# VectorE's adjacency offsets: one fifteen-word register load a round against four loads of up to four words

## The chip, the cores and the metric

The kernel runs on one core of one Trainium2 chip. The metric is the device time of one execution in microseconds. Before the change the median of three runs is 1594.96 us (1593.28 to 1598.29).

## The reference, cut to what matters

There are 3125 nodes with 128 features and 100000 edges, sorted by destination. Two graph layers follow one another, each with a residual and a layer norm.

```python
# layer 0: max over the incoming edges of a linear message
msgs = z[edge_dst] @ Wd + z[edge_src] @ Ws + edge_weight[:, None] * ww[None, :] + bm
agg = jax.ops.segment_max(msgs, edge_dst, num_segments=n)
x = _layernorm(x + relu(z @ W1a + agg @ W1b + b1) @ W2 + b2)
# layer 1: two SAGE convolutions, each with the mean over the incoming edges
agg = jax.ops.segment_sum(x[src], dst, num_segments=n)
mean = agg / jnp.maximum(deg, 1.0)[:, None]
x = _layernorm(x + conv2(relu(conv1(x))))
```

## The kernel before, in words

The kernel has three parts in time. First a setup sorts out where edges and nodes lie. Then the gather pass `gather_pass(0)` computes the segment maximum of layer 0, and beside it builds the adjacency matrix as counts in SBUF (`adj`, bf16). Then the dense tail runs the layers; the second layer's sums are matmuls with that adjacency matrix.

The change is in the gather pass. It has 49 rounds (`ROUNDS`). A round has 16 steps (`RING`), in four blocks of four (`NB`, `BS`). In each block:

- GpSimd gathers four sets of 128 rows by indirect DMA (L651), after ScalarE has copied the indices (L486).
- ScalarE computes the weighted part of four messages (L496).
- VectorE waits for the gathered rows (`landed`, L826) and for ScalarE (`weighed`, L828), adds the two for the whole block (L830), waits for the end of its own addition (`summed`, L831), and then runs four steps. A step is one running maximum (L841); steps are chained by the semaphore `stepped` (L840).

In the first 47 rounds (`PROUNDS`) the first 15 steps (`RP`) of a round also take a pair each, 705 pairs in all. A pair stands for one batch of 256 edges and one window of ten destination nodes. VectorE and ScalarE make one-hot matrices for it (L855 and L857 on VectorE, L526 and L535 on ScalarE), TensorE multiplies them into a PSUM bank (L1123), and three steps later (`LAG`) VectorE adds the product into 250 columns of the adjacency matrix (`add_product`, L861 to L866). Which columns these are is known only at run time: the start is a number that VectorE's sequencer reads into a register. The numbers lie in SBUF in `offw`, 16 words to a round (`OFFW`), fifteen of them used.

The load of these registers is L836, `values_load_multi_w_load_instructions`, in `turn` of VectorE's `gather_pass`. It stands in the loop over the steps, where `j % OFFS == 0`, ahead of the wait and the step L841 of the same j. With `OFFS = 15` that is j = 0 alone: one load of fifteen words a round, behind the wait for `summed` of the first block. After the 47 rounds another load of three words (L879) serves the last three products. One further register load is used in the trace as a measure: L283 reads one word on each engine to choose the form of the second layer.

All of the order is written out by hand; each engine executes its own list, and the loops over the rounds are real loops with a register counter. So the column of `nlo`, `key`, `keep` and the waited values are computed by register instructions on the engine's sequencer. In the trace these stand as DVEq, VectorE's sequencer.

The constants that matter:

```python
RP = 15
LAG = 3
OFFS = 15
OFFW = 16
```

Of the kernel before, what the change touches and what calls it, by code (L numbers as in the profile page):

```python
# [52 lines left out]
RP = 15  # L53
PR = 5
LAG = 3
OFFS = 15
OFFW = 16
WINDOWS = ("COLS times a pair's window, which is the number of NWIN ordered window starts at or before the pair, less "
           "one; the first of them is pair 0")
# [25 lines left out]
def gnn_kernel(nc, x, src, dst, w, Wm, bm, W1, b1, W2, b2, W1lT, b1l, W1rT, W2lT, b2l, W2rT, out):  # L85
# [16 lines left out]
    with ctx:  # L102
# [96 lines left out]
        offw = off.rearrange("p r c -> p (r c)")  # L199
# [492 lines left out]
        def _(dve):  # L692
# [123 lines left out]
            def gather_pass(q):  # L816
# [6 lines left out]
                def turn(i, first, pairs):  # L823
                    offs = []
                    for b in range(NB):
                        dve.wait_ge(landed[b], q * ROUNDS * BS * 16 + 16 * BS * i + 16 * BS)  # L826
                        if q == 0:
                            dve.wait_ge(weighed, i * NB + b + 1)  # L828
                            part = runs[:, b * BS:(b + 1) * BS, :]
                            nc.vector.tensor_tensor(part, part, gath[:, b * BS:(b + 1) * BS, :], ALU.add).then_inc(summed, 1)  # L830
                            dve.wait_ge(summed, i * NB + b + 1)  # L831
                        elif not first:
                            dve.wait_ge(dumped[b], q * ROUNDS * 16 + 16 * i)
                        for j in range(b * BS, (b + 1) * BS):
                            if pairs and j < RP and j % OFFS == 0:
                                offs += nc.values_load_multi_w_load_instructions(  # L836
                                    offw[0:1, bass.ds(i * OFFW + j, OFFS)], engines=[mybir.EngineType.DVE],
                                    min_val=0, max_val=(NWIN - 1) * COLS, skip_runtime_bounds_check_because=WINDOWS)[1]
                            if not (first and j == 0):
                                dve.wait_ge(stepped, q * CHUNK + i * RING + j)  # L840
                            nc.vector.scalar_tensor_tensor(  # L841
                                runs[:, j, :], runs[:, (j - 1) % RING, :], mask[:, bass.ds(i * RING + j, 1)],
                                (runs if q == 0 else gath)[:, j, :], op0, op1).then_inc(stepped, 1)
                            if pairs and j < RP:
                                one_hots(i, j, first)
                                if not (first and j < LAG):
                                    add_product(offs[j], i * RP + j - LAG, (j - LAG) % PR, first and j == LAG)

                def one_hots(i, j, first):
                    s = j % PR  # L850
                    if not (first and j < PR):
                        dve.wait_ge(paired, i * RP + j - PR + 1)
                    for u in range(SUB):
                        if j not in BY_ACT:
                            nc.vector.tensor_scalar(hot_l[:, s, u * P:(u + 1) * P], niota_l[:, :],  # L855
                                                    nlo[:, u, bass.ds(i * RP + j, 1)], None, ALU.is_equal)
                        last = nc.vector.tensor_scalar(hot_d[:, s, u * COLS:(u + 1) * COLS], iota_d[:, :],  # L857
                                                       key[:, u, bass.ds(i * RP + j, 1)], None, ALU.is_equal)
                    last.then_inc(made_d, 1)

                def add_product(at, n, s, alone):  # L861
                    dve.wait_ge(paired, n + 1)
                    if not alone:
                        dve.wait_ge(added, n)
                    a = adj[:, bass.ds(at, COLS)]
                    nc.vector.tensor_tensor(a, bank[s][:, 0:COLS], a, ALU.add).then_inc(added, 1)  # L866

                if q == 0:
                    dve.wait_ge(zeroed[0], 16)
                turn(0, True, q == 0)  # L870
                if q == 0:
                    with dve.Fori(1, SAFE) as i:
                        turn(i, False, True)
                    with dve.Fori(SAFE, SAFE + ZROUNDS) as i:
                        dve.wait_ge(zeroed[1], i * 16 - (SAFE - 1) * 16)
                        turn(i, False, True)
                    with dve.Fori(SAFE + ZROUNDS, PROUNDS) as i:
                        turn(i, False, True)
                    offs = nc.values_load_multi_w_load_instructions(  # L879
                        offw[0:1, PROUNDS * OFFW:PROUNDS * OFFW + LAG], engines=[mybir.EngineType.DVE], min_val=0,  # L880
                        max_val=(NWIN - 1) * COLS, skip_runtime_bounds_check_because=WINDOWS)[1]
                    for k in range(LAG):
                        add_product(offs[k], PAIRS - LAG + k, (PAIRS - LAG + k) % PR, False)
# [390 lines left out]
```

## Time and profile before

| | |
|---|---|
| median of three runs | 1594.96 us |
| lowest and highest | 1593.28 and 1598.29 us |
| the profiled execution's own time | 1589.41 us |
| its span in the profile | 1587.6 us |
| VectorE busy | 1087.8 us |
| ScalarE busy | 884.1 us |
| GpSimd busy | 845.0 us |
| TensorE matmul busy | 835.7 us |
| granted TensorE clock, mean | 0.622 of full speed |

The profile comes from one execution. Its span is from the first to the last instruction; the execution's own time is 1.8 us longer. Busy time counts work on data only: register loads, register arithmetic, branches and waits are not in it. They are seen as DVEq rows of the chain that ended last and of a single line's view, and as idle time of the engine, where "issue" names idle time that no semaphore of another instruction explains.

### The profile page before, as it was taken

To read this page: it belongs to the slowest core of one execution; us is meant where nothing else is said; L and a number is where in the kernel's file an instruction comes from. 1 tells how busy PE (TensorE), PEld (TensorE's weight loads), DVE (VectorE), ACT (ScalarE), POOL (GpSimd) and SP (SyncE) were. 2 spreads that over 40 slices of the span, in tenths; PEclk is the share of its full clock that TensorE was granted. 3 is DMA by queue.
4 is the path that set the end of the run, shared out by engine and by line. 5 is a ranking of instruction groups with operands and counts; after the bars stand their busy time and mean duration, and the time that the engine had idled before them with its cause. 6 is when DMAs were issued, how large, how long until landed. Compare 5 with 4: busy or idle time off the path is not lost.

```text
span 1587.6 us, 27890 instructions
## 1 busy us (share of the span) xinstructions
PE 835.7 (53%) x3528; PEld 428.8 (27%) x3528; DVE 1087.8 (69%) x3961; ACT 884.1 (56%) x2856; POOL 845.0 (53%) x851
## 2 busy tenths in 40 slices
PE   0473444443444444444444444444409969999898
PEld 0441000000000000000000000000006748887687
DVE  3368888888888888898888898888843341112433
ACT  0117787777787777777777877777711130001200
POOL 1056777777777777777777777777755000000000
PEclk9785555555555555555555555555556579999899
DMA  2583444444443333333333333333342231111211
GB/s 81 168 296 119 134 155 146 143 149 130 140 150 96 94 95 101 95 94 101 94 96 94 101 96 94 99 96 96 99 129 76 67 92 40 41 40 41 65 34 30
DMA packets 114997, 163.01 MB, mean 103 GB/s; under 512 B 20330, under 2 KB 74013, under 8 KB 114954
## 3 DMA queue, kind: packets, MB, share of 16 engines
q1 hardware_dynamic: 86276, 99.13, 18.5%
q0 software_dynamic: 27952, 63.24, 14.5%
q8 instruction: 19, 0.31, 0.1%
q10 hardware_dynamic: 726, 0.13, 0.1%
q14 instruction: 24, 0.20, 0.0%
HBM read 79.07 MB, written 63.28 MB: 90 GB/s over the span
## 4 chain that ended last, share of the span: by engine, by line
DVE 36%; PE 21%; issue 17%; DVEq 15%; DMA 6%; SPq 3%; ACT 1%; POOL 1%; POOLq 0%; ACTq 0%
PE bank L1229 12%; DVE late L857 11%; DVE rings L830 8%; DVE adj_w L866 7%; DVEq L836 6%; DVE rings L841 5%; DVEq L857 3%; DVE late L855 2%; DMA adj_w<-dst_d,adj_w 2%; DVEq L841 2%; PE bank L1202 2%; SPq L312 2%; DMA dst_d<-adj_w 2%; PE bank L1169 1%; DVEq L866 1%
## 5 line engine op out<-in xcount | busy, mean ns | idle before, releaser
L651 POOL DMA_INDIRECT rings<-zs_d,idx x784 | 790.3, 1008 | 270.8 <-issue 246.9
L1123 PE MATMUL bank<-late 128*128 128x250 bf16 x1410 | 421.3, 402 | 602.5 <-DVE late L857 591.5
L526 ACT ACTIVATE late<-late 128x128 bf16<-128x128 bf16 x1128 | 367.5, 388 | 24.1
L857 DVE TENSOR_SCALAR late<-late 128x250 bf16<-128x250 bf16 x1410 | 374.1, 310 | 0.0
L841 DVE SCALAR_TENSOR_TENSOR rings<-rings,keep 128x128 f32<-128x128 f32 x784 | 269.6, 344 | 140.4 <-issue 103.8
L1123 PEld LDWEIGHTS bank<-late 128*128 128x128 bf16 x1410 | 93.2, 111 | 930.2 <-DVE late L857 581.4
L866 DVE TENSOR_TENSOR adj_w<-bank,adj_w 128x250 f32 x705 | 287.4, 408 | 0.9 <-DVE adj_w L866 0.4
L535 ACT ACTIVATE late<-late 128x256 bf16<-128x256 bf16 x564 | 223.8, 405 | 90.3 <-PE bank L1123 90.3
L496 ACT ACTIVATE rings<-ww,late 128x128 f32<-128x128 f32 x784 | 250.3, 390 | 1.6 <-DVE rings L841 1.6
L1229 PE MATMUL bank<-rings,adj_w 128*128 128x384 bf16 (+1 forms) x1250 | 214.3, 332 | 20.7 <-DVE rings L1007 20.7
L1229 PEld LDWEIGHTS bank<-rings,adj_w 128*128 128x128 bf16 (+1 forms) x1250 | 180.9, 149 | 51.5 <-DVE rings L1007 29.2
L830 DVE TENSOR_TENSOR rings<-rings 128x512 f32<-128x512 f32 x196 | 132.8, 678 | 9.2 <-DMA rings<-zs_d,idx 9.1
L577 ACT ACTIVATE late<-bank,cols 128x256 f32<-128x256 f32 (+1 forms) x39 | 16.8, 464 | 181.4 <-PE bank L1170 181.4
L486 ACT COPY idx<-src_i 128x4 int32 (+1 forms) x196 | 37.7, 193 | 139.8 <-DVE rings L841 103.5
L965 DVE COPY late<-bank 128x256 f32<-128x256 f32 (+1 forms) x13 | 5.4, 415 | 116.4 <-PE bank L1205 116.4
L855 DVE TENSOR_SCALAR late<-late 128x128 bf16<-128x128 bf16 x282 | 76.3, 272 | 0.0
L1021 DVE TENSOR_REDUCE late<-bank 128x128 f32<-128x384 f32 (+1 forms) x50 | 26.8, 554 | 63.2 <-PE bank L1229 61.0
L642 POOL DMA_INDIRECT adj_w<-dst_d,adj_w x25 | 23.8, 951 | 85.4 <-DMA dst_d<-adj_w 69.0
L557 ACT ACTIVATE sd<-mv,eps 128x2 f32<-128x2 f32 (+1 forms) x26 | 7.7, 297 | 93.3 <-DVE mv L923 93.3
L783 DVE TENSOR_SCALAR_CACHE_REDUCE adj_w<-adj_w 128x784 f32<-128x784 f32 x25 | 25.7, 1029 | 33.6 <-DMA adj_w<-dst_d,adj_w 33.4
L476 ACT COPY adj_w<-bank 128x256 f32<-128x256 f32 (+1 forms) x13 | 4.7, 365 | 70.5 <-PE bank L1081 48.3
L913 DVE TENSOR_TENSOR late<-rings,bank 128x256 f32<-128x256 f32 (+1 forms) x13 | 5.3, 411 | 44.5 <-PE bank L1146 33.5
(157 smaller groups left out, 600.0 us busy)
## 6 DMA issues: line engine op xcount, KB each, us to landing
run_d<-rings SPq DMA_DIRECT2D x196, 256.0 KB, 2.1
adj_w<-zeros SPq DMA_DIRECT2D x16, 980.0 KB
rings<-zs_d,idx POOLq DMA_INDIRECT x784
adj_w<-zeros SPq DMA_DIRECT2D x1, 3920.0 KB, 24.4
late<-x_d SPq DMA_DIRECT2D x24, 128.0 KB, 2.3
xT_d<-adj_w SPq DMA_DIRECT2D x12, 128.0 KB, 6.8
zs_d<-adj_w SPq DMA_DIRECT2D x12, 128.0 KB, 6.5
late<-xT_d SPq DMA_DIRECT2D x12, 128.0 KB, 2.2
```

The costliest lines, as they stand in the source:

```text
L496: last = nc.scalar.activation(runs[:, b * BS + j, :], ww[:, :], ACT.Copy, scale=w_s[:, bass.ds(i * RING + b * BS + j, 1)])
L526: last = nc.scalar.activation(a[:, u * P:(u + 1) * P], iota_l[:, :], ACT.Square, bias=nlo[:, u, bass.ds(i * RP + j, 1)])
L535: nc.scalar.activation(hot_l[:, s, :], sq[:, n % 2, :], ACT.Relu, bias=1.0, scale=-1.0).then_inc(made_l, 1)
L651: pool.indirect_dma_start(gath[:, j, :], None, table, bass.IndirectOffsetOnAxis(ap=idx[:, j:j + 1], axis=0), compute_op=ALU.bypass).then_i ...
L830: nc.vector.tensor_tensor(part, part, gath[:, b * BS:(b + 1) * BS, :], ALU.add).then_inc(summed, 1)
L836: offs += nc.values_load_multi_w_load_instructions(offw[0:1, bass.ds(i * OFFW + j, OFFS)], engines=[mybir.EngineType.DVE], min_val=0, max_ ...
L841: nc.vector.scalar_tensor_tensor(runs[:, j, :], runs[:, (j - 1) % RING, :], mask[:, bass.ds(i * RING + j, 1)], (runs if q == 0 else gath)[ ...
L855: nc.vector.tensor_scalar(hot_l[:, s, u * P:(u + 1) * P], niota_l[:, :], nlo[:, u, bass.ds(i * RP + j, 1)], None, ALU.is_equal)
L857: last = nc.vector.tensor_scalar(hot_d[:, s, u * COLS:(u + 1) * COLS], iota_d[:, :], key[:, u, bass.ds(i * RP + j, 1)], None, ALU.is_equal)
L866: nc.vector.tensor_tensor(a, bank[s][:, 0:COLS], a, ALU.add).then_inc(added, 1)
L1123: last = nc.tensor.matmul(bank[s][:, 0:COLS], hot_l[:, s, u * P:(u + 1) * P], hot_d[:, s, u * COLS:(u + 1) * COLS], start=u == 0, stop=u = ...
L1229: return nc.tensor.matmul(bank[ADJ_BANKS[t % 3]][0:k, 0:3 * F], adj_v[:, t * P:t * P + k, h], parts[:, h, :], start=h == 0, stop=h == NT - 1)
```

## The change

The group of a load becomes four words instead of fifteen, and the last load of a round takes the three that remain. So in each of the 47 rounds there are four loads, of 4, 4, 4 and 3 words, at j = 0, 4, 8 and 12. Each is the first step of a block, so that each load stands behind that block's wait for `summed`. The 3-word load at L879 stays as it is.

```diff
-OFFS = 15
+OFFS = 4
...
                             if pairs and j < RP and j % OFFS == 0:
                                 offs += nc.values_load_multi_w_load_instructions(
-                                    offw[0:1, bass.ds(i * OFFW + j, OFFS)], engines=[mybir.EngineType.DVE],
+                                    offw[0:1, bass.ds(i * OFFW + j, min(OFFS, RP - j))], engines=[mybir.EngineType.DVE],
                                     min_val=0, max_val=(NWIN - 1) * COLS, skip_runtime_bounds_check_because=WINDOWS)[1]
```

## Rows read from the trace of the kernel before

**Rows 1.** The profile's first two parts: busy time of the engines, and the 40 slices.

```profile
span 1587.6 us, 27890 instructions
PE 835.7 (53%) x3528; PEld 428.8 (27%) x3528; DVE 1087.8 (69%) x3961; ACT 884.1 (56%) x2856; POOL 845.0 (53%) x851
...
DVE  3368888888888888898888898888843341112433
...
PEclk9785555555555555555555555555556579999899
```

**Rows 2.** Busy time by stretch: stretch, its length, PE, PEld, DVE, ACT, POOL, clock, DMA.

```profile
129.00:1148.00 1019.00, 420.68 (x1408) 93.03 (x1408) 883.49 (x3333) 808.87 (x2636) 760.93 (x754) 0.50 0.36 112
1148.00:1182.00 34.00, 1.04 (x3) 0.32 (x3) 18.90 (x46) 8.14 (x29) 21.78 (x22) 0.50 0.34 106
```

**Rows 3.** VectorE's waits from 129 to 1148 us: total us, times, longest.

```profile
DVE rings L841 <- issue: 103.8, 47, 2.3
DVE rings L841 <- DVE rings L830: 31.4, 138, 0.2
DVE adj_w L866 <- issue: 0.2, 1, 0.2
```

**Rows 4.** Timeline of VectorE: two loads one round apart, and a block without one.

```profile
608.06 0.35 DVE L841 SCALAR_TENSOR_TENSOR rings<-rings,keep 128x128 f32<-128x128 f32 x1 [2.22 <-issue]
...
613.23 0.35 DVE L841 SCALAR_TENSOR_TENSOR rings<-rings,keep 128x128 f32<-128x128 f32 x1 [0.23 <-DVE rings L830]
...
629.73 0.35 DVE L841 SCALAR_TENSOR_TENSOR rings<-rings,keep 128x128 f32<-128x128 f32 x1 [2.22 <-issue]
```

**Rows 5.** Chain that ended last, 626 to 630 us: start, us, what.

```profile
626.82 0.69 DVE rings L830
627.52 0.03 issue
627.55 0.08 DVEq L836
627.63 0.03 issue
627.66 1.93 DVEq L836
629.59 0.05 issue
629.64 0.05 DVEq L841
```

**Rows 6.** Line L836: durations ns min/median/max, first and last start.

```profile
L836 DVEq TENSOR_LOAD <-late x47: 1800/1922/2050, 129.5 to 1127.6; - x47
L836 DVEq FUSED_REGOPS  x46: 64/81/81, 149.3 to 1127.5; - x46
```

**Rows 7.** Lines L879 and L283, same columns: register loads of three and one words.

```profile
L879 DVEq TENSOR_LOAD <-late x1: 767/767/767, 1147.9 to 1147.9; - x1
...
L283 DVEq TENSOR_LOAD <-large x1: 439/439/439, 1283.2 to 1283.2; - x1
```

**Rows 8.** Timeline of VectorE around the three-word load.

```profile
1147.89 0.40 DVE L866 TENSOR_TENSOR adj_w<-bank,adj_w 128x250 f32 x1
1148.22 0.33 DVE L841 SCALAR_TENSOR_TENSOR rings<-rings,keep 128x128 f32<-128x128 f32 x1
1148.90 0.42 DVE L866 TENSOR_TENSOR adj_w<-bank,adj_w 128x250 f32 x1 [0.34 <-PE bank L1123]
```

**Rows 9.** Groups by line, 129 to 1148 us: busy, mean ns, idle before and releasers.

```profile
L651 POOL DMA_INDIRECT rings<-zs_d,idx x754 | 760.9, 1009 | 261.6 <-issue 239.0 <-ACT idx L486 22.6
L1123 PE MATMUL bank<-late 128*128 128x250 bf16 x1408 | 420.7, 402 | 602.1 <-DVE late L857 591.1 <-issue 8.1 <-ACT late L535 1.6
...
L535 ACT ACTIVATE late<-late 128x256 bf16<-128x256 bf16 x564 | 223.8, 405 | 90.3 <-PE bank L1123 90.3
...
L486 ACT COPY idx<-src_i 128x4 int32 (+1 forms) x188 | 36.3, 193 | 92.6 <-DVE rings L841 92.6
```

**Rows 10.** Timeline of GpSimd, one gather with the pause before it.

```profile
611.22 0.97 POOL L651 DMA_INDIRECT rings<-zs_d,idx  x1 [0.30 <-issue]
```

## The prediction, made before the changed kernel was run

> **What bounds the kernel now.** Read the slices first: VectorE is at eight or nine tenths in nearly all slices of the long middle, while TensorE's clock there stands at half, the lower of its two levels, 1.2 GHz [rows 1]. Then cut that middle out: from 129 to 1148 us, 1019 us long, VectorE works 883.5 us, more than any other engine [rows 2]. Its 135.5 us of idle time have two causes only [rows 3]: 103.8 us ahead of 47 maxima L841 with no releaser ("issue"), and 31.4 us ahead of 138 others, behind the block's addition L830. No wait for GpSimd, ScalarE or TensorE is among them. So the stage lasts as long as VectorE's list lasts, and whatever is added to that list where the engine is drained is added to the kernel.
>
> The 47 gaps are the register loads. Two of them lie 21.67 us apart (608.06 and 629.73), one round, each 2.22 us, while a block without a load has 0.23 us in that place [rows 4]. The chain shows what fills one: the addition ends, 0.03 us pass, 0.08 us of register arithmetic, 0.03 us, the load with 1.93 us, and then the step's own register work [rows 5]. The load begins only after the addition, since it stands behind the wait for `summed`. It is one instruction of fifteen words, 47 in all, 1800 to 2050 ns with a median of 1922 [rows 6].
>
> **What the change removes and adds.** It removes 47 loads of fifteen words and adds 141 of four words and 47 of three. The number of words is the same, so the question is what a load costs beside its words. The trace holds two shorter loads on the same sequencer: three words took 767 ns in the same stage, one word 439 ns later, in a quieter one [rows 7].
>
> The line through three and fifteen words has a slope of (1922 - 767) / 12 = 96 ns a word, and leaves 767 - 3 x 96 = 479 ns for the load itself. A load of four words is then 863 ns. I take this value, since it is one word away from the nearest row and both rows are from this stage. The four loads of a round take 3 x 863 + 767 = 3356 ns instead of 1922: 1.434 us more.
>
> Around a load there is more than its duration: the gap with one is 2.22 - 1.92 = 0.30 us longer than the load, where a plain gap has 0.23 [rows 4, 6]. That is the address arithmetic and its pause; three blocks get it anew, 3 x 0.07 = 0.21 us. A round grows by 1.434 + 0.21 = 1.64 us, and 47 rounds by **77.3 us**.
>
> The other edits have one answer: that the registers are loaded nearer to their use gives nothing, because an offset is first needed by L866, which never waits for it; L879 is unchanged.
>
> **Bounds of the unknown term.** The four-word load isn't in the trace. From below: the line through one and fifteen words has a slope of (1922 - 439) / 14 = 106 ns, so 757 ns for four words and 651 for three. The sum is 3 x 757 + 651 - 1922 = 1000 ns, with the 0.21 us 1.21 us a round, 56.9 us. (This takes the single three-word row to be an outlier.) From above: the line through one and three words has 164 ns a word, so 931 ns for four: 3 x 931 + 767 - 1922 = 1638 ns, with the 0.21 us 1.85 us a round, 86.9 us. A gain from the loads themselves is excluded by these rows: even one word costs more than 3 x 96 ns.
>
> A rule bears on this. The trace has 439 ns for a one-word load, and a fixed part near 480 by the line above [rows 7]. The Trainium skill, "DMA: Bandwidth & Descriptors", section "Latency and other measured facts", gives a register load from memory (`tensor_load`) a floor of about 600 ns, to be spread over several words; the rule speaks against this change, and by its 600 ns for each of the three extra loads the estimate would be 3 x 0.6 + 0.21 = 2.01 us a round, 94.5 us in all, or 1689 us. By the trace the floor is lower, and the trace's value is the one used.
>
> **What could hide it, and what waits behind it.** Each new load sits behind the wait for `summed`, so VectorE has nothing queued ahead of it: no cover. Queued behind it are the block's four maxima, its one-hots and the products' additions. TensorE waits for those one-hots; it idles 602 us before L1123 already, 591 us of it for VectorE's L857. ScalarE waits 92.6 us for VectorE at L486 and 90.3 us for TensorE at L535. The gathers wait 22.6 us for L486 [rows 9]. All three get more slack, none becomes late. TensorE's clock is at its lower level through the stage and can't fall; the dense tail is untouched. In the 34 us after the pairs VectorE works 18.9 us and isn't the limit [rows 2]; nothing there changes. So the 77.3 us go straight into the time.
>
> **The sum.** The profiled execution took 1589.41 us (span 1587.6): it would become 1666.7 us. It lies 5.55 us under the median of 1594.96, by which I go: 1594.96 + 77.3 = **1672.3 us**.
>
> **The rivals.**
>
> *A load costs by the word alone.* Then splitting moves the fifteen words about, 1.92 us a round as before, and only the 3 x 0.07 us are new: 47 x 0.21 = 9.9 us, 1604.8 us. Against it: per word, fifteen cost 128 ns each, three 256 and one 439 [rows 6, 7]. For it: the two short loads are one row each. Chance 0.03. The Trainium skill, "Runtime: NRT & Kernel Launch", section "Instruction fetch mechanics", states about 200 ns a register even for bulk loads, a price by the word alone, from another memory than here. By that rule fifteen words would be an estimated 3.0 us, and the trace disagrees with its 1.92.
>
> *The new loads run under other work, and the kernel becomes faster.* The sequencer can run ahead: the three-word load began at 1147.9 us, while VectorE worked on L866 and then L841 up to 1148.55 [rows 7, 8], and next to nothing of it showed. If the loads of the second to fourth block did so, only the first would stay open, with four words: 1.92 - 0.86 = 1.06 us less a round, 49.8 us. GpSimd would stop it sooner: 760.9 us of gathers and a pause of 0.30 us before nearly each (726 of them counted in its issue waits) make 979 us of the 1019 [rows 2, 9, 10], so at most 40 us go, to 1555 us. The point that decides is whether a load starts before its block's L830 ends. Against it: L879 has no `summed` wait ahead of it, whereas the load in the loop does, and each of the two gaps shown begins with L830's end [rows 4, 5]. Chance 0.03.
>
> *The loads are dearer than above.* Four words near 1.1 us, or a restart of the sequencer that shows at later steps as well: over 86.9 us, from 1686 us on. For it: loads in the stage vary by 250 ns [rows 6]. Chance 0.07.
>
> *Something of both signs cancels* to within 0.3%, such as half-covered loads: 0.01.
>
> **How the numbers follow.** The forecast has what is left, 0.86, with its time of 1672.3. Its range goes by the bounds: 1593.28 + 56.9 = 1650 and 1598.29 + 86.9 = 1685, a little wider for the small terms, 1648 to 1686. This leaves out the first two rivals and the dearer loads, about 1 in 7 with the edges. Against no change, 0.3% (5 us) is what a measurement of this kernel can tell. Faster: the covered loads, 0.03. Same: 0.01. Slower: all the rest, 0.96.
>
> **What would show it.** In the profile of after, L836 has 188 register loads, 141 near 860 ns and 47 near 770. The waits of VectorE have L841 behind "issue" 188 times (or under L830's name), each 1.0 to 1.2 us, 214 us or so in place of 135.5. The distance from one round's first L841 to the next is 23.3 us instead of 21.67. Busy times stay as they were, and the stage that began at 129 us ends near 1225. I am wrong if four-word loads are far from 860 ns, if they begin before L830 ends, or if VectorE begins to wait for GpSimd, ScalarE or TensorE.

## The result, and the profile after

The changed kernel takes 1613.04 us (median of four runs, 1605.51 to 1614.01), the kernel before 1594.12 us beside it. The ratio is 1.0104, 95% interval 1.0068 to 1.0141: slower by 1.0%, which is 18.9 us. The forecast was 1672.3 us with a range from 1648 to 1686. The direction was right, the size four times too large, and the result lies outside the range.

The page of the profile after, the lines that answer to [rows 1]:

```profile
span 1610.3 us, 28166 instructions
PE 841.7 (52%) x3528; PEld 433.1 (27%) x3528; DVE 1085.2 (67%) x3961; ACT 891.7 (55%) x2856; POOL 838.6 (52%) x851
```

The loads of line L836 after (durations ns min/median/max, first and last start), which answer to [rows 6]:

```profile
L836 DVEq TENSOR_LOAD <-late x188: 339/346/767, 129.5 to 1162.1; - x188
L836 DVEq FUSED_REGOPS  x184: 57/57/81, 149.8 to 1162.0; - x184
```

VectorE's waits after, from 129 to 1165 us (total us, times, longest), which answer to [rows 3]:

```profile
DVE rings L841 <- DVE rings L830: 98.8, 137, 0.9
DVE rings L841 <- issue: 56.8, 51, 1.4
DVE adj_w L866 <- issue: 0.2, 1, 0.2
```

The 188 loads are there, and VectorE still waits for nobody else. The idle time ahead of L841 went from 135.2 to 155.6 us, 20.4 more, which is the whole change within the spread of the runs. But a load has a median of 346 ns, where 863 were forecast for four words. The chain that ended last shows one in the second block of a round (start, us, what):

```profile
619.88 0.61 DVE rings L830
620.49 0.03 issue
620.52 0.06 DVEq L836
620.58 0.04 issue
620.61 0.34 DVEq L836
620.96 0.03 issue
620.99 0.04 DVEq L840
621.03 0.05 issue
621.08 0.05 DVEq L841
621.13 0.05 issue
621.18 0.10 DVE rings L841
```

It stands where the forecast put it, right behind L830. Read the four gaps of a round in the timeline of VectorE after:

```profile
604.74 0.35 DVE L841 SCALAR_TENSOR_TENSOR rings<-rings,keep 128x128 f32<-128x128 f32 x1 [0.70 <-DVE rings L830]
...
610.79 0.35 DVE L841 SCALAR_TENSOR_TENSOR rings<-rings,keep 128x128 f32<-128x128 f32 x1 [1.10 <-issue]
...
615.50 0.35 DVE L841 SCALAR_TENSOR_TENSOR rings<-rings,keep 128x128 f32<-128x128 f32 x1 [0.81 <-DVE rings L830]
...
621.18 0.35 DVE L841 SCALAR_TENSOR_TENSOR rings<-rings,keep 128x128 f32<-128x128 f32 x1 [0.69 <-DVE rings L830]
```

In the order of time these are the third and fourth block of one round and the first and second of the next. They sum to 3.30 us, against 2.22 + 3 x 0.23 = 2.91 before [rows 4]: 0.39 us a round, 18.3 us in 47 rounds. The odd one is the 1.10: it belongs to the smallest load, the one of three words, 0.75 us in the chain at 609.82, while the loads of four words beside it take 0.34 (at 604.17), 0.52 (614.84) and 0.34 (620.61). Three words cost twice what four do. A cost that is a fixed part and a price a word can't do that, and this is where the experiments began.

### The profile page after: what moved, and what is told of

It is laid out like the page before. It is cut to its first block, busy times and chain, and to the rows that moved or that the text cites. A ratio compares the mean times of both kernels' runs of the same rounds, so it can differ in the third digit from the quotient of the medians.

```text
span 1610.3 us, 28166 instructions
## 1 busy us (share of the span) xinstructions
PE 841.7 (52%) x3528; PEld 433.1 (27%) x3528; DVE 1085.2 (67%) x3961; ACT 891.7 (55%) x2856; POOL 838.6 (52%) x851
## 3 DMA queue, kind: packets, MB, share of 16 engines
q1 hardware_dynamic: 86276, 99.13, 18.3%
## 4 chain that ended last, share of the span: by engine, by line
DVE 36%; PE 23%; issue 16%; DVEq 15%; DMA 5%; SPq 3%; ACT 1%; POOL 1%; POOLq 0%; ACTq 0%
PE bank L1229 12%; DVE late L857 12%; DVE rings L830 8%; DVE adj_w L866 7%; DVEq L836 6%; DVE rings L841 5%; DVEq L857 3%; DVE late L855 3%; DVEq L866 2%; DMA adj_w<-dst_d,adj_w 2%; PE bank L1123 2%; DVEq L841 2%; PE bank L1202 2%; PE bank L1169 2%; SPq L312 2%
## 5 line engine op out<-in xcount | busy, mean ns | idle before, releaser
L841 DVE SCALAR_TENSOR_TENSOR rings<-rings,keep 128x128 f32<-128x128 f32 x784 | 269.5, 344 | 160.7 <-DVE rings L830 100.6
L857 DVE TENSOR_SCALAR late<-late 128x250 bf16<-128x250 bf16 x1410 | 365.9, 305 | 0.0
L866 DVE TENSOR_TENSOR adj_w<-bank,adj_w 128x250 f32 x705 | 286.8, 407 | 0.9 <-DVE adj_w L866 0.4
L535 ACT ACTIVATE late<-late 128x256 bf16<-128x256 bf16 x564 | 227.2, 407 | 68.0 <-PE bank L1123 57.1
L830 DVE TENSOR_TENSOR rings<-rings 128x512 f32<-128x512 f32 x196 | 132.9, 678 | 8.0 <-DMA rings<-zs_d,idx 7.9
L642 POOL DMA_INDIRECT adj_w<-dst_d,adj_w x25 | 23.8, 952 | 85.5 <-DMA dst_d<-adj_w 68.8
```

The source lines that it names most:

```text
L535: nc.scalar.activation(hot_l[:, s, :], sq[:, n % 2, :], ACT.Relu, bias=1.0, scale=-1.0).then_inc(made_l, 1)
L841: nc.vector.scalar_tensor_tensor(runs[:, j, :], runs[:, (j - 1) % RING, :], mask[:, bass.ds(i * RING + j, 1)], (runs if q == 0 else gath)[ ...
```

## The experiments

Three theories of a load's duration stood to begin with: **A**, it is read in pieces, a full group of four words being one cheap piece and each word left over a piece of its own; **B**, a size that is a multiple of four goes a fast way as a whole; **C**, the line of the prediction holds, and the short loads have another reason.

### e1: the sizes side by side

```diff
                     dve.wait_ge(added, PAIRS)
+                    at = nc.values_load_multi_w_load_instructions(
+                        offw[0:1, 0:1], engines=[mybir.EngineType.DVE], min_val=0, ...)[1][-1]
+                    link(nc.vector.tensor_copy(st[0:1, 0, 0, 0:1], adj[0:1, bass.ds(at, 1)]))
...
                     link(nc.vector.memset(tN[:, :, :, :], 0.0))
```

> The kernel before, with 34 more register loads on VectorE after the last product, each followed by a one-element copy that uses the value and is waited for: sizes 1, 2, 3, 4, 5, 6, 7, 8, 9, 12, 15 and 16 words from a start that is a multiple of 16 bytes, then 4 words from one and two words later, 8 from two later, 3 and 1 from one later; twice. The output is unchanged. Theory A (a load is read in pieces: each full four words is one piece of about 350 to 390 ns, each word left over about 160, with some 280 for these together): 4 words 350, 5 words about 800, 8 words 700 to 780, 7 words 1150, 12 words 1050 to 1150, 15 words 1920, 16 words 1400 to 1560. Theory B (a load whose size is a multiple of four goes a fast way as a whole, any other goes word by word with 100 to 160 ns a word): 8, 12 and 16 words under 700 ns, 5 words about 1000, 7 words about 1200, 15 words 1920. Theory C (the line of the prediction, 479 ns and 96 a word; the 346 ns of the changed kernel have another reason): 8 words 1250, 16 words 2010. If the start matters, 4 words from an odd word cost as 3 do or more (over 750 ns).

Single lines' views of the kernel with the scan; here 1, 3, 4, 5, 7, 8, 12, 15 and 16 words from word 0, then 4 words from word 1, and 8 from word 2:

```profile
L956 DVEq TENSOR_LOAD <-late x1: 318/318/318, 1201.0 to 1201.0; - x1
L964 DVEq TENSOR_LOAD <-late x1: 741/741/741, 1202.5 to 1202.5; - x1
L968 DVEq TENSOR_LOAD <-late x1: 357/357/357, 1203.5 to 1203.5; - x1
L972 DVEq TENSOR_LOAD <-late x1: 610/610/610, 1204.2 to 1204.2; - x1
L980 DVEq TENSOR_LOAD <-late x1: 1035/1035/1035, 1206.2 to 1206.2; - x1
L984 DVEq TENSOR_LOAD <-late x1: 606/606/606, 1207.6 to 1207.6; - x1
L992 DVEq TENSOR_LOAD <-late x1: 857/857/857, 1209.6 to 1209.6; - x1
L996 DVEq TENSOR_LOAD <-late x1: 1542/1542/1542, 1210.8 to 1210.8; - x1
L1000 DVEq TENSOR_LOAD <-late x1: 1104/1104/1104, 1212.6 to 1212.6; - x1
L1004 DVEq TENSOR_LOAD <-late x1: 973/973/973, 1214.1 to 1214.1; - x1
L1012 DVEq TENSOR_LOAD <-late x1: 1842/1842/1842, 1216.6 to 1216.6; - x1
```

The kernel ran once, and this is its second pass through the sizes; the first gave the same within 10 ns, but for the three words (841 ns there). The numbers follow theory A with other prices. The step from 4 to 8, 12 and 16 words is 247 to 251 ns each. A word left over costs 212 to 253 (4 to 5, 5 to 7, 12 to 15 words). So a load is about 107 ns, plus 250 for each full group of four, plus 216 for each other word; this gives the eleven rows within 40 ns. (It is fitted to these rows; e2, e3 and e13 to e15 test it in the time.) A group counts only where the load starts on the grid of four words: 4 words from word 1 are 107 + 4 x 216 = 971 (973 measured), 8 from word 2 are 1835 (1842), although the words 4 to 7 among them lie on the grid. B falls with 12 and 16 words at 857 and 1104 ns, where it wants less than 700, and with 5 words at 610, where it wants about 1000; C with 3 words over 4, and with 15 over 16.

### e2 and e3: one word more

```diff
 # e2, from the changed kernel
-offw[0:1, bass.ds(i * OFFW + j, min(OFFS, RP - j))]
+offw[0:1, bass.ds(i * OFFW + j, OFFS)]
 # e3, from the kernel before
-offw[0:1, bass.ds(i * OFFW + j, OFFS)]
+offw[0:1, bass.ds(i * OFFW + j, OFFW)]
```

> The changed kernel with its last load of a round lengthened from three words to four (the word past the fifteen is the unused one, zero). Theory A and B: the 47 loads of 757 ns become 346 ns, 0.41 us less a round, 19 us less in all: 1594 us, as the kernel before. Theory C: one word more, 4 to 5 us slower than the changed kernel.

> The kernel before with its one load of a round lengthened from fifteen words to sixteen. Theory A: 1922 ns become 1400 to 1560, 17 to 25 us faster than before (1570 to 1578 us). Theory B: 1922 become under 700, 57 us less on VectorE's list, of which some 40 show before the gathers bound (1555 us or so). Theory C: 96 ns more in each of 47 rounds, 1599 us.

e2 took 1590.09 us against 1592.89 of the kernel before beside it, ratio 0.9992 (0.9968 to 1.0017): the change's 1.0% is gone by reading one word more. e3 took 1575.00 us, ratio 0.9906 (0.9871 to 0.9942): one load of sixteen words is 18 us faster than one of fifteen. The rows of L836, e2 and then e3, and e3's waits from 129 to 1123 us:

```profile
L836 DVEq TENSOR_LOAD <-late x188: 340/345/693, 129.7 to 1143.8; - x188
```

```profile
L836 DVEq TENSOR_LOAD <-late x47: 1357/1416/1553, 130.7 to 1103.5; - x47
```

```profile
DVE rings L841 <- issue: 80.9, 47, 1.9
DVE rings L841 <- DVE rings L830: 31.5, 138, 0.2
```

In e3 (1922 - 1416) x 47 = 23.8 us less of loads were to come, and the idle time ahead of L841 fell by 22.8 us to 112.4. e3 lies in theory A's range of 1570 to 1578 us and against B's 1555 and C's 1599. e2 is 4 us below the 1594 that A and B share, inside its own spread of 1587 to 1599, and against C, which wanted it slower than the changed kernel.

### e4: the loads beside the addition

```diff
                             nc.vector.tensor_tensor(part, part, gath[:, b * BS:(b + 1) * BS, :], ALU.add).then_inc(summed, 1)
+                            if pairs:
+                                offs += nc.values_load_multi_w_load_instructions(
+                                    offw[0:1, bass.ds(i * OFFW + b * BS, BS)], engines=[mybir.EngineType.DVE], ...)[1]
                             dve.wait_ge(summed, i * NB + b + 1)
...
-                            if pairs and j < RP and j % OFFS == 0:
-                                offs += ...
```

> Four loads of four words a round, each issued between the block's addition L830 and the wait for its end, so that it can run under the addition's 0.68 us. If VectorE's sequencer reads its registers while the engine computes, the whole load cost goes: every gap before L841 is 0.23 us again, VectorE's list is 94 us shorter than before, and the gathers bound the stage at about 979 us of 1019: 1555 us, 40 less than before. If the loads wait for the engine to drain in any case, the time is that of four exposed loads, 1594 us.

1540.91 us, ratio 0.9678 (0.9641 to 0.9714): 52 us faster than before, and the fastest kernel of this study. e2 has the same four loads of four words behind the wait and took 1590.09 us, so 49 us of it come from the place alone. Its waits from 129 to 1084 us:

```profile
DVE rings L841 <- DVE rings L830: 39.5, 138, 0.6
DVE rings L830 <- DMA rings<-zs_d,idx: 21.0, 48, 0.6
```

All "issue" gaps ahead of L841 are gone, and 135.2 - 39.5 = 95.7 us of idle time with them. The sequencer reads its registers while the engine adds. What bounds next is seen in the second line: L830 now waits for the gathers, 48 times. The three-word load L879, which ends the stage, starts at 1084.5 us instead of 1147.9, 63.4 us earlier. The forecast of this run, 1555, was too high, since it took the gathers at the 1009 ns of [rows 9]; they ran at 972 on the average here. Of the 63.4 us part is given back in the dense tail. The first row is the kernel before, the second e4, each for 108 us from shortly after the pass (stretch, length, PE, PEld, DVE, ACT, POOL, clock, DMA):

```profile
1182.00:1290.00 108.00, 89.55 (x303) 63.95 (x303) 36.60 (x133) 18.62 (x53) 25.55 (x27) 0.61 0.31 88
```

```profile
1120.00:1228.00 108.00, 94.86 (x285) 67.83 (x285) 35.88 (x125) 16.64 (x46) 25.73 (x27) 0.53 0.28 80
```

In e4 the clock stayed at its lower level longer after the pass (0.53 against 0.61 of full speed), and from L879 to the end it needed 1539.9 - 1084.5 = 455.4 us against 439.7. In that time TensorE was busy for 376.4 us against 365.9 with the same matmuls within two, so 10.5 of the 15.7 us lie in slower matmuls. Why the clock rose later wasn't tested.

### e5 to e8, e9 to e12: the same kernels where something else stops VectorE

Three kernels were to show the pieces in the time: e5 starts the four-word loads one word off the grid, e6 has two loads of eight words, e7 fifteen loads of one word. e8 repeats the scan right behind the rounds. e9 to e11 are e5 to e7 again, and e12 is the kernel before with only the place of its load changed, as in e4.

```diff
 # e5 and e9, from the changed kernel (and L771 to L775, L879 accordingly)
-offw[0:1, bass.ds(i * OFFW + j, min(OFFS, RP - j))]
+offw[0:1, bass.ds(i * OFFW + 1 + j, min(OFFS, RP - j))]
 # e6 and e10, from the changed kernel: OFFS = 8, all eight words read
 # e7 and e11, from the changed kernel: OFFS = 1
 # e12, from the kernel before: the load of fifteen words between L830 and the wait for summed
```

> The changed kernel with the offsets of a round kept one word later in their row of sixteen (words 1 to 15 instead of 0 to 14), so that its four loads start 4 bytes off the 16-byte grid; sizes 4, 4, 4 and 3 as before. Theory P (whole groups of four words are read as one piece only where they start on the 16-byte grid, everything else word by word): the three four-word loads take about 970 ns each instead of 346, the three-word one stays near 750; 3 x 0.62 = 1.87 us more a round, 88 us in all: 1700 us, near what was forecast for the change or over it. Theory C (the four-word load is cheap wherever it starts, and the slow ones of the scan had another reason): 1613 us, as the changed kernel.

> Two loads of eight words a round, at j = 0 and 8 (the last word unused). Theory P: each load is two pieces, 600 ns if a piece after the first takes 250 as in the quiet scan, 690 ns if it takes 340 as the 16-word load of e3 suggests (1416 = 346 + 3 x 357). In all 1.2 to 1.38 us a round and 0.12 for handling one more load, against 1.42 in e3: 1567 to 1579 us, the time of e3 within 6. A theory in which a load has a large fixed part of its own (some 480 ns, as the prediction had it) wants 0.5 us a round more than e3: 1598 us.

> Fifteen loads of one word a round, each just ahead of its step; four of them stand behind a block's wait for its own addition, eleven in the middle of a block, where VectorE still has work. If a load in mid-block is covered by the engine's work, only four show, each about 310 ns and 0.12 around it: 1.7 us a round against 1.99, 1580 to 1585 us. If VectorE's sequencer has no lead in mid-block (the chain there is full of its own register instructions), all fifteen show: 15 x (0.31 + 0.12) = 6.5 us a round, 4.5 more than before, 1800 us. In between, each covered in part.

> The kernel before with 14 register loads put right behind the 47 rounds with pairs, while gathers and stores still run: 16, 15, 12, 8, 4, 3 and 1 words on the 16-byte grid, twice, each followed by a waited one-element copy. It asks why fifteen words take 1922 ns in the rounds and 1542 in the quiet scan, and sixteen 1416 against 1105. If the gathers and stores alone slow the pieces after the first, 16 words take 1350 to 1550 here and 15 take 1800 to 2050. If it is something of the rounds (ScalarE's and TensorE's work, or a load whose address comes from a register), they take 1105 and 1542 as in the quiet scan.

> The kernel of e5 once more: there the kernel before itself took 1936 us, with VectorE stopped for 0.3 to 2.5 us at many other instructions, so that a load's cost could lie inside such a stop. Where the kernel before takes its usual 1593 us: theory P (read word by word off the 16-byte grid) wants three four-word loads of about 970 ns each, 1700 us; theory C (cheap wherever it starts) 1613 us.

> The kernel of e6 once more, where the kernel before takes its usual 1593 us. Theory P: two loads of 600 to 690 ns and 0.12 us for handling one more, 1567 to 1579 us. A theory with a large fixed part in each load: 1598 us.

> The kernel of e7 once more, where the kernel before takes its usual 1593 us. Loads in mid-block covered: 1580 to 1585 us. VectorE's sequencer without a lead in mid-block: 1800 us. In between, each covered in part.

> The kernel before with its one load of fifteen words issued between the block's addition and the wait for its end, nothing else. If the load runs beside the addition, some 0.60 us of its 1.92 are hidden in each of 47 rounds, 28 us: 1566 us. If it waits for the engine to drain: 1594 us, as before.

On the two chips that these ran on, the kernel before itself took 1936.02 us (e5 to e8) and 1897.92 us (e9 to e12) instead of 1593. e8 ran once, in 1936.84 us, and e11 twice. The ratios were 0.9908 (0.9878 to 0.9939) for e5, 1.0048 (1.0029 to 1.0067) for e6, 1.0008 (0.9974 to 1.0042) for e7, then 1.0024 (0.9993 to 1.0055), 1.0038 (1.0005 to 1.0071), 1.0109 (1.0007 to 1.0211) and 1.0032 (1.0004 to 1.0061) for e9 to e12. None is what a theory wanted, but for e12, whose 1.0032 looks like the "as before" of a load that waits for the engine; its trace, below, says otherwise. The costs of loads vanished from the time. The groups of e8's stage, where the rounds are those of the kernel before, show where VectorE stood still:

```profile
L866 DVE TENSOR_TENSOR adj_w<-bank,adj_w 128x250 f32 x701 | 287.8, 411 | 156.4 <-issue 128.8 <-PE bank L1179 24.2 <-remote 3.0
L841 DVE SCALAR_TENSOR_TENSOR rings<-rings,keep 128x128 f32<-128x128 f32 x751 | 259.4, 345 | 198.4 <-issue 161.0 <-DVE rings L830 23.4 <-PE bank L1179 7.9
```

L866, which waited 0.2 us in all before [rows 3], has 128.8 us of "issue" time, and L857, which had none, 61.9. VectorE's instruction stream stopped in the midst of blocks, for up to 3.2 us at a time. The stage from 129 us to L879's place is 1334.7 us long instead of 1018.9, and of the 316 us more some 250 are "issue" idle time and 32 waits for TensorE. What stops the stream on these chips is not shown by the profile and stays open. A load that falls into such a stop would cost nothing; that this is how the differences vanished is an argument only. The durations of the loads are of use all the same, though by their medians alone (single rows there are as short as 4 ns): 965 and 964 ns for the shifted loads, 303 for one word, and for eight words 604 in e10 but 794 in e6, since half of these loads belong to a first block and are dearer than the others. In e8, with the gathers still running, sixteen words took 1128 and 1106 ns as in the quiet scan, fifteen 1939 and 1552: the gathers alone don't slow them, and the 1939 stays unexplained.

e12's time hides what its trace shows. Here is the addition of a first block and the maximum behind it:

```profile
607.34 0.69 DVE L830 TENSOR_TENSOR rings<-rings 128x512 f32<-128x512 f32 x1
...
609.48 0.39 DVE L841 SCALAR_TENSOR_TENSOR rings<-rings,keep 128x128 f32<-128x128 f32 x1 [1.45 <-issue]
```

The gap is 1.45 us instead of 2.22 [rows 4], and its median over the 47 rounds 1.50, while the load keeps its length (median 1883 ns). So the fifteen-word load ran beside the addition too, for some 0.7 us a round; only the 33 us that this is didn't reach the time of this chip.

### e13 to e15: the pieces in the time

The three kernels of e5 to e7 ran once more, beside a kernel before of 1594.72 us.

> Third try for the kernel of e5, if the kernel before takes its 1593 us. Its three four-word loads took 965 ns (median) in e5 and e9. If that cost stands in VectorE's path: 3 x (965 - 346) = 1.86 us more a round than the changed kernel, 87 us, 1700 us. If the start did not matter in time: 1613 us.

> Third try for the kernel of e6, if the kernel before takes its 1593 us. Its eight-word loads took 604 ns (median) in e10. Two of them and 0.12 us for one more load to handle are 1.33 us a round against 1.42 in e3: 1571 us, the time of e3 less 4. With a large fixed part in each load: 1598 us.

> Third try for the kernel of e7, if the kernel before takes its 1593 us. The one-word loads took 303 ns. Four exposed and eleven covered: 1580 to 1585 us. All fifteen exposed: 15 x (0.30 + 0.12) = 6.3 us a round, 4.3 more than before, 1795 us.

**e13** took 1732.67 us, ratio 1.0863 (1.0823 to 1.0903). It has the same number of loads of the same sizes as the changed kernel, and is 7.5% slower than that, because they start 4 bytes further on. Its loads, and its waits from 129 to 1290 us:

```profile
L836 DVEq TENSOR_LOAD <-late x188: 740/966/2921, 130.8 to 1286.9; - x188
```

```profile
DVE rings L841 <- issue: 278.5, 187, 3.4
DVE rings L841 <- DVE rings L830: 0.8, 1, 0.8
```

279.3 us of idle time against 155.6 after the change, 123.7 more, where the sum expected 87. The rest is loads beyond 966 ns: in the first block they took 1.21 to 1.44 us, and in the second block 1.83 to 2.92 us in each of the first sixteen rounds, then 0.96 in all others. Some 25 us come from these sixteen loads. The price of single words doesn't explain them, and their cause stays open. This kernel lies beyond the 1686 us of the range: with loads off the grid the forecast would have been too low.

**e14** took 1580.39 us, ratio 0.9923 (0.9896 to 0.9949), 5 us more than e3, with intervals that overlap. The forecasts were 1571 and, with a large fixed part, 1598; it lies between them, 9 us over the first. Of its two loads the one in the first block took 0.97 us and the one in the third 0.60, as in the chain at 600.98 and 612.38, and the forecast had 0.60 for both. Two loads instead of one cost 124.0 - 112.4 = 11.6 us of idle time ahead of L841, where a fixed part of 480 ns would cost 23 and the handling besides.

**e15** took 1727.32 us, ratio 1.0836 (1.0799 to 1.0874). Neither end came true, but it is near the one with all loads exposed. The four gaps behind L830 are no longer than before in sum (0.90 and three of 0.67 are 2.91 us). The 133 us came from the eleven loads in mid-block. Here are two steps of e15 in the timeline, which lie 1.20 us apart where the kernel before has 0.97 to 1.01:

```profile
611.05 0.35 DVE L841 SCALAR_TENSOR_TENSOR rings<-rings,keep 128x128 f32<-128x128 f32 x1
611.32 0.48 DVE L857 TENSOR_SCALAR late<-late 128x250 bf16<-128x250 bf16 x2
611.71 0.41 DVE L866 TENSOR_TENSOR adj_w<-bank,adj_w 128x250 f32 x1
612.25 0.36 DVE L841 SCALAR_TENSOR_TENSOR rings<-rings,keep 128x128 f32<-128x128 f32 x1
```

132.6 us over 47 x 11 loads are 0.26 us for each load of 0.30. In mid-block the sequencer is hardly ahead of its engine, so that a load shows nearly whole. The view of waits makes this easy to miss: it names 136.9 + 39.1 = 176.0 us ahead of L841, 40.8 more than before. The groups of the stage have it all, first the kernel before and then e15, with e15's stretch to set beside [rows 2]:

```profile
L841 DVE SCALAR_TENSOR_TENSOR rings<-rings,keep 128x128 f32<-128x128 f32 x751 | 258.1, 344 | 135.3 <-issue 103.8 <-DVE rings L830 31.4
```

```profile
L841 DVE SCALAR_TENSOR_TENSOR rings<-rings,keep 128x128 f32<-128x128 f32 x751 | 263.8, 351 | 221.3 <-DVE rings L830 136.9 <-issue 39.1
```

```profile
129.00:1284.80 1155.80, 421.13 (x1409) 92.93 (x1410) 930.84 (x3334) 813.80 (x2637) 769.61 (x755) 0.50 0.31 99
```

The idle time ahead of L841 grew by 86.0 us, much of it in gaps of 0.1 us, and VectorE's busy time by 47.3 us to 930.8, although its instructions are no longer in sum: they overlap less. In the kernel before a maximum starts 0.08 us ahead of the end of the L866 before it (608.73 + 0.42 against 609.07); in e15 it starts 0.13 us behind it.

## Why the prediction was wrong, point by point

**Where the time is.** Right: VectorE bounds the stage, the loads stand in the open behind `summed`, nobody else begins to wait, and the added idle time (20.4 us) is the added time (18.9 us).

**The step that failed** is "A load of four words is then 863 ns", and with it the lower bound of 757. It measured 346. The line through the three-word and the fifteen-word load took the size as a number of words. In truth both rows hold the same three left-over words. Their difference, 1922 - 767 = 1155 ns, is three full groups of four, about 250 each by e1, and some 380 by which fifteen words take longer in the rounds than in the quiet scan (1922 against 1542), whose cause stays open. Most of the 479 ns that the line left "for the load itself" was the price of left-over words. The sum for a round then is 1.95 us of loads (0.52, 0.34, 0.34 and 0.75) against 1.92, in place of 3.36. This takes 1.41 x 47 = 66 us off the forecast. Fifteen words had been three groups and three singles all along; the change cut the load where it was cut already.

**The handling** of a new load was taken at 0.07 us and is 0.12: 0.81 - 0.52, 0.69 - 0.34, 0.70 - 0.34 and 1.10 - 0.75 sum to 1.35 us beside the loads, against 0.99 before. The chain shows a difference: behind the load comes L840's register arithmetic of 0.04 us and a pause, which the load of the first block doesn't have (its chain goes on with L841 at once, [rows 5]). This added 0.15 x 47 = 7 us. So 77.3 - 66 + 7 = 18 us, what was measured.

**The bounds** were both drawn through rows of leftovers, so neither was one. The one-word row of the lower one, 439 ns, reads another tile, and the same load took 581 ns in the changed kernel and one word of the offsets 318 in e1. "A gain from the loads themselves is excluded by these rows" was too strong also: e14 has two loads of eight words a round and is faster than one of fifteen.

**The rivals.** The price "by the word alone" came nearest with 1604.8 us, by chance: its reason, 128 ns a word, is wrong (e3 reads one word more and is 18 us faster; e13 reads the same words and is 8.6% slower than before). That loads could run under other work was refuted for this change, as forecast, and e4 and e12's trace show that the mechanism is there once the load stands ahead of the wait. The 600 ns floor from the Trainium skill ("DMA: Bandwidth & Descriptors", "Latency and other measured facts") was further off than the line: one word took 318 ns and four 357 in e1. The same row of the Trainium skill has compilers unroll such loads four times to amortize the floor; it names no cheap group of four words, which is what the traces show. The 200 ns a register of the Trainium skill, "Runtime: NRT & Kernel Launch", "Instruction fetch mechanics", agree with the 216 of a word left over, not with the 250 of a full group of four.

## What to carry to other kernels

Two measured durations make a line only if the cost is a line: ask what pieces the sizes are made of, and distrust a fixed part found by extrapolation. On VectorE here, pad a register load to a full multiple of four words on a 16-byte start; a word more can be 18 us less. Above all, put it between an instruction of the engine and the wait for that instruction, where it is hidden for as long as that instruction runs (e4, e12), and not into a dense run of instructions with register operands, where nearly all of it showed (e15).

## What was not expected of the hardware

- A register load costs less for four words (357 ns) than for two (541) or three (741), and a start off the 16-byte grid makes it 973 (e1).
- One load takes different times in different places, for a reason that stays open. In the changed kernel the first block's four words took 0.40 to 0.55 us in 29 of the last 30 rounds, but 0.34 in all but three of the seventeen before. In e14 eight words took 0.85 to 1.10 us in the first block and 0.60 in the third; fifteen took 1.92 in the rounds against 1.54 in e1, sixteen 1.42 against 1.10. It isn't tied to the first block: in e4 the first block's load took 0.34 us and the second block's mostly 0.72, in e13 the second block's took over 1.8 in sixteen rounds, and in e8 one load of fifteen words behind the rounds took 1.94.
- The same kernel took 1593, 1898 and 1936 us on three chips, with most of the extra time in "issue" stops of VectorE (e8). The fast one gave 1593 and 1595 us before and after the two slow ones were used. Each slow chip was used once, so that the chip is the cause, and not the hour, isn't shown. A difference between two kernels there, such as e5's 0.9908, says nothing of another chip.
